# Deformable-convolution block: both horizontal weights of a sample applied on ScalarE, mixing one tap earlier, row combinations spread over the strip

## The chip, the cores and the metric

The kernel runs as one program on one core of a Trainium2 chip. A core has five engines that run on their own and meet only at semaphores: TensorE (PE, matmuls; PEld are its weight loads), VectorE (DVE), ScalarE (ACT), GpSimd (POOL) and SyncE (SP), which only issues transfers here. The metric is the device time of one execution in microseconds (us), lower is better.

## The reference, cut to what matters

```python
out_normal = _conv(x, w_normal)                      # x is (4, 128, 80, 80), all convolutions 3x3
offset = concatenate([_conv(x, w_offx), _conv(x, w_offy)], axis=1)
out_x = _deform_conv(x, offset, w_dx)
out_y = _deform_conv(x, offset, w_dy)
out = _conv(concatenate([out_normal, out_x, out_y], axis=1), w_fusion)
out = relu(_bn(out, ...bn1)); out = _bn(_conv(out, w_conv2), ...bn2)
return relu(out + x)

# _deform_conv, for each of 9 taps: a position per pixel, and the four cells around it
s = corner(y0i, x0i, (1 - ty) * (1 - tx)) + corner(y0i, x0i + 1, (1 - ty) * tx) \
  + corner(y0i + 1, x0i, ty * (1 - tx)) + corner(y0i + 1, x0i + 1, ty * tx)
return einsum('bckhw,ock->bohw', s, wr)              # zero outside the image
```

## The kernel before, in words

**Tiling.** The four images are cut into 40 strips of 8 rows (640 pixels, 5 tiles of 128). The 9 taps of all strips are numbered through: tap n = 9 * strip + k. A sample of a tap needs four cells; each tile of 128 pixels is fetched by one gather on POOL (L352, `cells`, 2 KB for each pixel, 45 gathers a strip, 1800 in all), into 15 slots that are used in turn. For the first image the gather reads `xpair` (upper and lower row of a cell pair); for images 2 to 4 it reads `slope_table`, which the kernel itself writes during the first image and which holds the upper row and the difference of lower and upper, so that one VectorE instruction does the vertical mix.

**A sample** is made so. First image: `upper` on ACT (L537, `mixed<-cells`, 5 instructions of 256 columns) times 1-ty, then the VectorE mix. All images: VectorE mixes vertically (L754, 5 instructions of 128x256, into `mixed`, two buffers), ACT multiplies the left half by 1-tx (L537, `samp<-mixed`, 5 of 128x128), VectorE adds the right half times tx (L760, 5 of 128x128). PE turns the five tiles (L433, into the one PSUM buffer `turned`), ACT takes the high part of the result (L536, `samp_hi`), VectorE the low part (L706, `samp_lo`), and PE multiplies the tap for both deformable convolutions (`deform_tap`, 36 matmuls into `acc`).

**The step.** `step(i)` is written once for each engine and runs 44 times (40 strips and 4 steps that empty the pipeline); it goes through the 9 taps. At tap n PE turns tap n+1, works off the slices of `SLICES[k]`, and then does `deform_tap` n. The slices are parts of the plain convolutions of other strips: O (offsets of strip i+1), F (fusion of strip i-2, in four quarters), N (normal convolution of strip i), C (second convolution of strip i-4). They share the two PSUM banks `work[0]` and `work[1]`, so a slice waits until ACT or VectorE has emptied its bank. At tap n VectorE makes sample n+2 (mix, then sum), then `samp_lo` n+1, then what the slices finished at this tap. ACT does the left products of n+2, `samp_hi` n+1, `upper` n+3, then its share of the finished slices. Each engine works its list off in the order written; nothing overtakes.

**Row combinations.** When the last quarter of F is done (tap 6), VectorE forms sums, differences and shifted differences of the rows of strip i-1 (L834, L835, L836, L840), the low part of `mid` (L919) and the low parts of the combinations (L706 twice), one after another, and ACT the high parts between them.

**What holds a gather.** Gather number q waits until the mix has freed its slot (at least q-14 mixes done) and until PE has marked progress (`pace`, 5 marks a tap; at least q-24 marks). The gathers of a strip also wait for its indices (`indices`, L723 to L740, 13 small VectorE instructions on the turned offsets), made at tap 3 of the strip before.

Of the kernel before, what the change touches and what calls it, by code (L numbers as in the profile page):

```python
# [15 lines left out]
TAPS = 9  # L16
EPS = 1e-5
ROWS = 8
# [44 lines left out]
STEPS = NS + 4  # L63


SLICES = [
# [41 lines left out]
class Flags:  # L108


    def __init__(self, i):
# [14 lines left out]
        self.turn = 2 if first else 3  # L126
# [19 lines left out]
def deform_block(nc, x, xflat, xpair, weights, bn, const, out):  # L146
    ctx = ExitStack()
    with ctx:
# [39 lines left out]
        resid = sb("resid", [128, 2, PIX])  # L188
# [3 lines left out]
        off_f = sb("off_f", [128, TILES, OFFC])  # L192
# [44 lines left out]
        sums_done, sums_hi, sums_lo = sem("sums_done"), sem("sums_hi"), sem("sums_lo")  # L237
        zs_done, zs_hi, zs_lo = sem("zs_done"), sem("zs_hi"), sem("zs_lo")
# [6 lines left out]
        resid_in = [sem("resid_in0"), sem("resid_in1")]  # L245
        out_ready = sem("out_ready")
        out_stored = [sem("out_stored0"), sem("out_stored1")]
# [15 lines left out]
        fuse_mid = resid[:, :, :].rearrange("p a n -> p (a n)")[:, 0:9 * C].rearrange("p (g k) -> p g k", g=3)  # L263
# [7 lines left out]
        def _(eng):  # L271
# [41 lines left out]
            def step(i, par, fl):  # L313
# [19 lines left out]
            for par in range(2):  # L333
                eng.wait_ge(out_stored[par], 16 * (NS // 2))
# [31 lines left out]
        def _(eng):  # L366
# [61 lines left out]
            def turn_samples(n, tp):  # L428

                at_least(eng, samp_done, TILES * n + TILES)  # L430
# [26 lines left out]
            def step(i, par, fl):  # L457
                early = i < FIRST_STEPS
                for k in range(TAPS):
# [9 lines left out]
                    for job, q, a, b in fl.slices[k]:  # L469
# [3 lines left out]
                        if a == 0 and job == "C":  # L473
# [4 lines left out]
                            if i - 1 < NS:  # L478
# [5 lines left out]
                        if a == 0 and job == "O":  # L484
                            if q == 0:
                                at_least(eng, x_lo_done, i + 2)
                            if not early:
                                at_least(eng, c_out, 2 * (i - 4) + q + 1)
                            elif i:
                                at_least(eng, n_out, 2 * (i - 1) + q + 1)  # L490
                            else:
                                at_least(eng, p_out, 1)
                        if a == 0 and job == "F":
                            if q == 0:
                                at_least(eng, w_lo_done, 1 + W_FUSE)
                                at_least(eng, sums_lo, i - 1)
                            if q == 2:
                                at_least(eng, zs_lo, i - 1)
# [4 lines left out]
                            if q < 2:  # L503
                                if not fl.nxt:
# [28 lines left out]
        def _(eng):  # L533
# [21 lines left out]
            def turned_evac(s):  # L555
                at_least(eng, p_done, s + 1)
                at_least(eng, idx_step, NIDX * (s - 1) + 2)
# [3 lines left out]
            def upper(n, c, k, par, tp):  # L561
                if c >= STRIPS:
                    return

                at_least(eng, samp_done, TILES * (n - 1))
                for j in range(TILES):
# [3 lines left out]
                         scale=wgt[:, par, 0, 0, j, k:k + 1]).then_inc(upper_done, 1)  # L570

            def left(n, k, par, tp):

                at_least(eng, samp_turned, n - 1)
# [25 lines left out]
            upper(0, 0, 0, 0, 0)  # L600
            left(0, 0, 0, 0)
            x_high(1, 1)
            upper(1, 0, 1, 0, 1)
            samples_high(0, 0)
            left(1, 1, 0, 1)
            upper(2, 0, 2, 0, 0)
# [5 lines left out]
            def rows_high(s):  # L612
# [382 lines left out]
```

## Time and profile before

| what | us |
|---|---|
| median of 3 runs (lowest, highest) | 2839.32 (2833.42, 2855.32) |
| the profiled execution | 2821.6 |
| its span, first to last instruction | 2819.8 |
| PE, PEld busy | 2410.5, 2374.3 |
| DVE busy | 2190.3 |
| POOL busy | 2160.5 |
| ACT busy | 1598.3 |

The profile is one execution; it took 0.6% less than the median of the runs. Busy is the time in which an engine has an instruction under way; an engine can be the bound with less than a full share if what it idles between two instructions is its own overhead. TensorE's granted clock was 0.933 of full speed in the mean.

### The profile page before, as it was taken

Reading aid. Unit: us, or ns where it says so; the run is one execution under the profiler, and the core shown is the slowest. Engines: PE = TensorE matmul, PEld = TensorE weight load, DVE = VectorE, ACT = ScalarE, POOL = GpSimd, SP = SyncE. Lnnn points to the kernel's source line nnn. Section 1 sums busy time; section 2 is a strip of 40 time slices with the busy share of each in tenths; the row PEclk is TensorE's granted clock in tenths of the full one; section 3 lists DMA queues with packets and bytes.
Section 4 is the critical chain, followed back from the end, with each engine's and each line's share of the span. In section 5 each row is a group of like instructions: output and inputs, shape, how many; then the busy total and the mean of one; then the engine's idle time right before and its main releaser. Section 6 shows DMA issues by size and latency. Waiting matters only on the chain.

```text
span 2819.8 us, 46173 instructions
## 1 busy us (share of the span) xinstructions
PE 2410.5 (85%) x15680; PEld 2374.3 (84%) x15680; DVE 2190.3 (78%) x5199; ACT 1598.3 (57%) x3577; POOL 2160.5 (77%) x1807
## 2 busy tenths in 40 slices
PE   3578889988988888888999888988999888888897
PEld 3577889888988888888998888988999888888897
DVE  5778778888877787777888877877878777778762
ACT  5777777877555555444555555555555555555541
POOL 7787777887777878888777788787777888777840
PEclk7789999999999999999999999999999999999999
DMA  7766777767766676666777766766666666666540
GB/s 228 210 209 209 218 223 214 218 208 217 215 219 215 198 232 205 202 201 199 221 229 221 224 198 211 230 184 192 197 199 194 180 184 184 191 198 206 175 135 20
DMA packets 179132, 564.84 MB, mean 200 GB/s; under 512 B 32720, under 2 KB 34128, under 8 KB 178768
## 3 DMA queue, kind: packets, MB, share of 16 engines
q0 software_dynamic: 144000, 471.97, 56.2%
q1 hardware_dynamic: 34896, 89.91, 9.1%
q8 instruction: 125, 2.05, 0.3%
q14 instruction: 111, 0.91, 0.1%
HBM read 527.41 MB, written 34.34 MB: 199 GB/s over the span
## 4 chain that ended last, share of the span: by engine, by line
PE 42%; DVE 24%; DMA 17%; issue 7%; ACT 5%; POOL 5%; ACTq 0%; POOLq 0%; DVEq 0%; SPq 0%
DMA cells<-slope_table,index 14%; PE work L390 9%; PE work L393 9%; PE work L396 9%; DVE mixed L754 5%; POOL cells L352 5%; PE turned L433 4%; DVE d_lo L706 4%; DVE samp L760 4%; PE acc L390 3%; PE acc L396 3%; PE acc L393 3%; DVE samp_lo L706 3%; DMA cells<-in_xpair,index 3%; DVE d_lo_f L836 2%
## 5 line engine op out<-in xcount | busy, mean ns | idle before, releaser
L352 POOL DMA_INDIRECT cells<-slope_table,index x1350 | 1627.7, 1206 | 411.3 <-issue 229.7
L537 ACT ACTIVATE samp<-mixed,wgt 128x128 f32<-128x128 f32 x1800 | 667.9, 401 | 784.7 <-DVE mixed L754 781.6
L754 DVE SCALAR_TENSOR_TENSOR mixed<-cells,wgt 128x256 f32<-128x256 f32 x1350 | 589.3, 479 | 324.8 <-DMA cells<-slope_table,index 322.2
L352 POOL DMA_INDIRECT cells<-in_xpair,index x450 | 523.1, 1162 | 144.9 <-issue 84.1
L433 PE MATMUL turned<-cst,samp 128*128 128x128 f32 x1800 | 283.9, 293 | 323.0 <-DVE samp_lo L706 302.1
L390 PE MATMUL work<-d_hi,w_hi 128*128 128x320 f32 x1440 | 475.5, 330 | 58.4 <-ACT off_s L536 52.2
L760 DVE SCALAR_TENSOR_TENSOR samp<-mixed,wgt,samp 128x128 f32<-128x128 f32 x1800 | 505.9, 344 | 21.6 <-ACT samp L537 21.2
L433 PEld LDWEIGHTS turned<-cst,samp 128*128 128x128 f32 x1800 | 229.3, 150 | 347.2 <-DVE samp L760 300.6
L393 PE MATMUL work<-d_lo,w_hi 128*128 128x320 f32 x1440 | 459.3, 319 | 0.0
L396 PE MATMUL work<-d_hi,w_lo 128*128 128x320 f32 x1440 | 458.8, 319 | 0.0
L390 PE MATMUL acc<-samp_hi,w_hi 128*128 128x320 f32 x1440 | 450.3, 313 | 1.0 <-DVE samp_lo L706 1.0
L393 PE MATMUL acc<-samp_lo,w_hi 128*128 128x320 f32 x1440 | 448.2, 311 | 0.0
L396 PE MATMUL acc<-samp_hi,w_lo 128*128 128x320 f32 x1440 | 448.0, 311 | 0.0
L706 DVE TENSOR_TENSOR samp_lo<-turned,samp_hi 128x640 fp32r<-128x640 f32 x360 | 294.1, 817 | 62.2 <-ACT samp_hi L536 61.3
L390 PEld LDWEIGHTS work<-d_hi,w_hi 128*128 128x128 f32 x1440 | 278.4, 193 | 68.2 <-ACT off_s L536 60.7
L536 ACT ACTIVATE samp_hi<-turned 128x640 fp32r<-128x640 f32 x360 | 249.2, 692 | 58.3 <-PE turned L433 56.2
L393 PEld LDWEIGHTS work<-d_lo,w_hi 128*128 128x128 f32 x1440 | 279.0, 194 | 0.0
L396 PEld LDWEIGHTS work<-d_hi,w_lo 128*128 128x128 f32 x1440 | 278.2, 193 | 0.0
L390 PEld LDWEIGHTS acc<-samp_hi,w_hi 128*128 128x128 f32 x1440 | 275.7, 191 | 1.2 <-DVE samp_lo L706 1.2
L393 PEld LDWEIGHTS acc<-samp_lo,w_hi 128*128 128x128 f32 x1440 | 274.4, 191 | 0.0
L396 PEld LDWEIGHTS acc<-samp_hi,w_lo 128*128 128x128 f32 x1440 | 273.4, 190 | 0.0
L390 PE MATMUL work<-x_hi,w_hi 128*128 128x320 f32 x720 | 259.7, 361 | 0.0
(89 smaller groups left out, 4166.8 us busy)
## 6 DMA issues: line engine op xcount, KB each, us to landing
cells<-slope_table,index POOLq DMA_INDIRECT x1350, 3.9
slope<-in_xpair SPq DMA_DIRECT2D x54, 384.0 KB, 5.6
slope_table<-slope SPq DMA_DIRECT2D x54, 384.0 KB
x_raw<-in_xflat SPq DMA_DIRECT2D x40, 410.0 KB, 4.3
resid<-in_x SPq DMA_DIRECT2D x40, 320.0 KB, 6.2
out<-resid SPq DMA_DIRECT2D x40, 320.0 KB, 4.0
cells<-in_xpair,index POOLq DMA_INDIRECT x450, 3.9
w_lo_f<-in_weights SPq DMA_DIRECT2D x4, 576.0 KB, 8.2
```

The source lines that it names most:

```text
L352: eng.indirect_dma_start(out=cells[:, g, :], out_offset=None, in_=cell_rows, in_offset=bass.IndirectOffsetOnAxis(ap=index[:, par, j, k:k + ...
L390: ins = eng.matmul(dst, w_hi[:, w], hi, start=start, stop=False, skip_group_check=True)
L393: ins = eng.matmul(dst, w_hi[:, w], lo, start=False, stop=False, skip_group_check=True)
L396: return eng.matmul(dst, w_lo[:, w], hi, start=False, stop=stop, skip_group_check=True)
L433: ins = eng.transpose(turned[:, j * 128:(j + 1) * 128], samp[:, tp, j, :], ident)
L536: return eng.activation(dst, src, ACT.Copy)
L537: return eng.activation(dst, src, ACT.Copy, scale=scale)
L706: return eng.tensor_tensor(dst, src, hi.bitcast(F32), ALU.subtract)
L754: eng.scalar_tensor_tensor(out=both, in0=corner[:, g, :, 1, :], scalar=wgt[:, par, 1, 0, j, k:k + 1], in1=base, op0=ALU.mult, op1=ALU.add, ...
L760: eng.scalar_tensor_tensor(out=samp[:, tp, j], in0=mixed[:, tp, j, C:2 * C], scalar=wgt[:, par, 1, 1, j, k:k + 1], in1=samp[:, tp, j], op0 ...
L836: eng.tensor_tensor(to[:, :, 1:Z_ROWS - 1, :], raw[:, :, 0:ROWS - 2, :], raw[:, :, 2:ROWS, :], ALU.subtract)\
```

## The change

- The descriptor scratch of the software-issued transfers (the gathers) goes from 4096 to 8192 bytes of each partition. To make room, `resid` has one buffer and not two, and the offset sum `off_f` is formed in place in `off_s`.
- For images 2 to 4 ACT makes both horizontal products, in place in `mixed` (10 instructions of 128x128 a tap, `across`), and VectorE adds the halves for all five tiles in one instruction of 128x640 (`blend`). The first image keeps the products and sums it had.
- At tap n VectorE does the sum of n+2, `samp_lo` n+1, and then the mix of n+3, one tap further ahead than before. ACT does `samp_hi` n+1 first, then the products of n+3 and `upper` n+4.
- The row combinations are spread: sums and differences at tap 4, their low part at tap 5, shifted differences at tap 6, their low part at tap 7. ACT's high parts move with them.
- From step 4 on the offsets O come first, whole, in tap 0; C follows in taps 0 to 2; F and N stand where they ended before. The offsets are turned at tap 1 (before 3). So C's first slice waits for the offsets' evacuation from the bank and not for N's.
- On SP the load of `resid` for a strip stands behind the store of the strip before and waits for it.

```diff
 SLICES = [
-    [("C", 0, 0, 9), ("C", 1, 0, 1)],
-    [("C", 1, 1, 9), ("O", 0, 0, 3)],
-    [("O", 1, 0, 3), ("F", 0, 0, 6)],
-    [("F", 0, 6, 9), ("F", 1, 0, 6)],
-    [("F", 1, 6, 9), ("F", 2, 0, 6)],
-    [("F", 2, 6, 9), ("F", 3, 0, 6)],
-    [("F", 3, 6, 9), ("N", 0, 0, 5)],
-    [("N", 0, 5, 9), ("N", 1, 0, 4)],
-    [("N", 1, 4, 9)],
+    [("O", 0, 0, 3), ("O", 1, 0, 3), ("C", 0, 0, 3)],
+    [("C", 0, 3, 9), ("C", 1, 0, 3)],
+    [("C", 1, 3, 9), ("F", 0, 0, 3)],
+    [("F", 0, 3, 9), ("F", 1, 0, 3)],
+    [("F", 1, 3, 9), ("F", 2, 0, 3)],
+    [("F", 2, 3, 9), ("F", 3, 0, 3)],
+    [("F", 3, 3, 9), ("N", 0, 0, 2)],
+    [("N", 0, 2, 9), ("N", 1, 0, 1)],
+    [("N", 1, 1, 9)],
 ]
...
-        self.turn = 2 if first else 3
+        self.turn = 2 if first else 1
...
-        resid = sb("resid", [128, 2, PIX])
+        resid = sb("resid", [128, PIX])
...
-                if fl.resid:
-                    s = i - 3
-                    slot = 1 - par
-                    at_least(eng, out_stored[slot], 16 * (s // 2))
-                    eng.dma_start(resid[:, slot], x[:, s * PIX:(s + 1) * PIX]).then_inc(resid_in[slot], 16)
                 if fl.second:
                     s = i - 4
                     at_least(eng, out_ready, 2 * s + 2)
-                    eng.dma_start(out[:, s * PIX:(s + 1) * PIX], resid[:, par]).then_inc(out_stored[par], 16)
+                    eng.dma_start(out[:, s * PIX:(s + 1) * PIX], resid[:]).then_inc(out_stored, 16)
+                if fl.resid:
+                    s = i - 3
+                    at_least(eng, out_stored, 16 * s)
+                    eng.dma_start(resid[:], x[:, s * PIX:(s + 1) * PIX]).then_inc(resid_in, 16)
...
-                            if i - 1 < NS:
+                            if fl.nxt and q == 0:
+                                at_least(eng, o_out, 2 * (i + 1) + 1)
+                            elif fl.nxt:
+                                at_least(eng, p_out, i + 2)
+                            elif i - 1 < NS:
                                 at_least(eng, n_out, 2 * (i - 1) + q + 1)
...
+            def across(n):
...
+                c, k, tp = n // TAPS, n % TAPS, n % 2
+                if n < PLAIN:
+                    at_least(eng, samp_turned, n - 1)
                 for j in range(TILES):
                     at_least(eng, mixed_done, TILES * n + j + 1)
-                    copy(samp[:, tp, j], mixed[:, tp, j, 0:C], scale=wgt[:, par, 0, 1, j, k:k + 1]).then_inc(left_done, 1)
+                    left, right = mixed[:, tp, j, 0:C], mixed[:, tp, j, C:2 * C]
+                    if n < PLAIN:
+                        copy(samp[:, tp, j], left, scale=wgt[:, c % 2, 0, 1, j, k:k + 1]).then_inc(left_done, 1)
+                    else:
+                        copy(left, left, scale=wgt[:, c % 2, 0, 1, j, k:k + 1]).then_inc(left_done, 1)
+                        copy(right, right, scale=wgt[:, c % 2, 1, 1, j, k:k + 1]).then_inc(left_done, 1)
...
-                    if fl.strip and k < TAPS - 2:
-                        left(n + 2, k + 2, par, tp)
...
                     if k == fl.turn and fl.nxt:
                         turned_evac(i + 1)
+                    across(n + 3)
+                    upper(n + 4)
...
+            def blend(n):
...
+                if n >= PLAIN:
+                    at_least(eng, samp_turned, n - 1)
+                    at_least(eng, left_done, left_count(n + 1))
+                    eng.tensor_tensor(samp[:, tp], mixed[:, tp, :, 0:C], mixed[:, tp, :, C:2 * C], ALU.add)\
+                        .then_inc(samp_done, 1)
+                    return
...
-                    if fl.strip and k < TAPS - 2:
-                        sample(n + 2, k + 2, par, tp)
...
+                    blend(n + 2)
                     if fl.strip and (k < TAPS - 1 or fl.nxt):
                         samples_low(n + 1, 1 - tp)
...
+                    mix(n + 3)
...
+                        if job == "F" and q == 1 and fl.rows:
+                            sums(i - 1)
...
+                        if job == "F" and q == 2 and fl.rows:
+                            sums_low(i - 1)
                         if job == "F" and q == T - 1:
...
                             if fl.rows:
-                                rows_combined(i - 1)
+                                zs(i - 1)
...
-                            if fl.rows:
-                                rows_low(i - 1)
+                        if job == "N" and q == 0 and fl.rows:
+                            zs_low(i - 1)
...
-    nc = bacc.Bacc("TRN2", target_bir_lowering=False, num_devices=1, dynamic_dma_scratch_size=4096)
+    nc = bacc.Bacc("TRN2", target_bir_lowering=False, num_devices=1, dynamic_dma_scratch_size=8192)
```

Two places of the order, in the middle of a strip of images 2 to 4. The first is VectorE's list from the last tap before the row combinations to the tap after them, before the change (L834 to L840 are the row combinations, L919 the low part of `mid`, L706 into `d_lo` the low parts, L870 a part of the slope table):

```order
L754 SCALAR_TENSOR_TENSOR mixed<-cells,wgt 128x256 x5
L760 SCALAR_TENSOR_TENSOR samp<-mixed,wgt,samp 128x128 x5
L706 TENSOR_TENSOR samp_lo<-turned,samp_hi 128x640
L870 TENSOR_TENSOR slope<-slope 128x3x128
L913 SCALAR_TENSOR_TENSOR mid_f<-work,minus,mid_f 128x4x80
L834 TENSOR_TENSOR d_lo_f<-raw 128x3x4x80
L835 TENSOR_TENSOR d_lo_f<-raw 128x3x4x80
L836 TENSOR_TENSOR d_lo_f<-raw 128x3x6x80
L840 TENSOR_TENSOR d_lo_f<-keep,raw 128x3x80
L919 SCALAR_TENSOR_TENSOR mid<-mid_f,mid 128x8x80
L706 TENSOR_TENSOR d_lo<-d_lo_f,d_hi 128x3x8x80
L706 TENSOR_TENSOR d_lo<-d_lo_f,d_hi 128x3x7x80
```

And the same list after it, from tap 4 to tap 6:

```order
L779 SCALAR_TENSOR_TENSOR mixed<-cells,wgt 128x256 x5
L948 SCALAR_TENSOR_TENSOR mid_f<-work,scale,mid_f 128x4x80
L950 SCALAR_TENSOR_TENSOR mid_f<-work,minus,mid_f 128x4x80
L875 TENSOR_TENSOR d_lo_f<-raw 128x3x4x80
L876 TENSOR_TENSOR d_lo_f<-raw 128x3x4x80
L792 TENSOR_TENSOR samp<-mixed 128x640
L728 TENSOR_TENSOR samp_lo<-turned,samp_hi 128x640
L779 SCALAR_TENSOR_TENSOR mixed<-cells,wgt 128x256 x5
L957 SCALAR_TENSOR_TENSOR mid_f<-work,scale,mid_f 128x4x80
L728 TENSOR_TENSOR d_lo<-d_lo_f,d_hi 128x3x8x80
L792 TENSOR_TENSOR samp<-mixed 128x640
L728 TENSOR_TENSOR samp_lo<-turned,samp_hi 128x640
```

The seven instructions that stood in one piece are now in four places, and between the mix and the next `samp_lo` there is one sum and not five. The second place is ACT's list from the end of a strip to tap 2 of the next, after the change:

```order
L549 ACTIVATE raw<-acc 128x320 x4
L549 ACTIVATE samp_hi<-turned 128x640
L550 ACTIVATE mixed<-mixed,wgt 128x128 x10
L549 ACTIVATE off_c<-work 32x320 x6
L549 ACTIVATE samp_hi<-turned 128x640
L549 ACTIVATE off_s<-work 128x270
L550 ACTIVATE mixed<-mixed,wgt 128x128 x10
L549 ACTIVATE d_hi<-d_lo_f 128x3x80
L710 ACTIVATE resid<-resid,scale 128x320
```

The evacuation of the offsets (`off_c`) stands behind the ten products of tap 0, in one piece, and every run of products stands behind the `samp_hi` of its own tap.

## Rows read from the trace of the kernel before

**Rows 1.** Page, costliest groups: busy, mean ns of one, idle before, its releasers.
```profile
L352 POOL DMA_INDIRECT cells<-slope_table,index x1350 | 1627.7, 1206 | 411.3 <-issue 229.7
L352 POOL DMA_INDIRECT cells<-in_xpair,index x450 | 523.1, 1162 | 144.9 <-issue 84.1
```

**Rows 2.** Windows, all engines: first image (late part), images 2 to 4.
```profile
381.60:678.50 296.90, 265.99 (x1747) 262.45 (x1747) 241.06 (x586) 232.52 (x550) 234.02 (x204) 0.95 0.72 223
678.50:2655.80 1977.30, 1746.57 (x11453) 1723.49 (x11452) 1580.31 (x3771) 1036.74 (x2280) 1578.46 (x1310) 0.95 0.67 204
```

**Rows 3.** Timeline of POOL: start, length, engine, line, operation, idle before and releaser.
```profile
886.45 8.75 POOL L352 DMA_INDIRECT cells<-slope_table,index  x1 [0.30 <-issue]
1642.00 8.75 POOL L352 DMA_INDIRECT cells<-slope_table,index  x1 [0.30 <-issue]
1651.06 2.99 POOL L352 DMA_INDIRECT cells<-slope_table,index  x1 [0.30 <-DVE mixed L754]
2655.78 9.53 POOL L352 DMA_INDIRECT cells<-slope_table,index  x1 [0.30 <-PE work L390]
```

**Rows 4.** Timeline of DVE at 1642: the row combinations and what follows.
```profile
1641.20 1.15 DVE L834 TENSOR_TENSOR d_lo_f<-raw 128x960 f32<-128x960 f32 x1
1649.85 2.06 DVE L754 SCALAR_TENSOR_TENSOR mixed<-cells,wgt 128x256 f32<-128x256 f32 x5
```

**Rows 5.** Timeline, POOL then DVE, at another strip's row combinations.
```profile
1030.81 2.32 POOL L352 DMA_INDIRECT cells<-slope_table,index  x1 [0.30 <-PE acc L390]
1033.43 2.81 POOL L352 DMA_INDIRECT cells<-slope_table,index  x1 [0.30 <-issue]
1036.55 1.52 POOL L352 DMA_INDIRECT cells<-slope_table,index  x1 [0.31 <-issue]
...
1032.23 0.40 DVE L840 TENSOR_TENSOR d_lo_f<-keep,raw 128x240 f32<-128x240 f32 x1
```

**Rows 6.** Timeline of POOL beside the mixes of other taps.
```profile
1523.97 3.26 POOL L352 DMA_INDIRECT cells<-slope_table,index  x1 [0.30 <-DVE mixed L754]
1615.29 0.95 POOL L352 DMA_INDIRECT cells<-slope_table,index  x1 [0.30 <-DVE mixed L754]
```

**Rows 7.** Timeline of DVE at those two places.
```profile
1523.03 2.06 DVE L754 SCALAR_TENSOR_TENSOR mixed<-cells,wgt 128x256 f32<-128x256 f32 x5
1526.32 0.82 DVE L706 TENSOR_TENSOR samp_lo<-turned,samp_hi 128x640 fp32r<-128x640 f32 x1
1615.41 0.48 DVE L754 SCALAR_TENSOR_TENSOR mixed<-cells,wgt 128x256 f32<-128x256 f32 x1 [0.18 <-DMA cells<-slope_table,index]
```

**Rows 8.** Timeline of ACT, then of DVE: a tap's chain, and a mix with its product.
```profile
1609.44 1.58 ACT L537 ACTIVATE samp<-mixed,wgt 128x128 f32<-128x128 f32 x5
1611.04 0.70 ACT L536 ACTIVATE samp_hi<-turned 128x640 fp32r<-128x640 f32 x1
1636.86 0.40 ACT L537 ACTIVATE samp<-mixed,wgt 128x128 f32<-128x128 f32 x1 [1.14 <-DVE mixed L754]
...
1611.78 0.82 DVE L706 TENSOR_TENSOR samp_lo<-turned,samp_hi 128x640 fp32r<-128x640 f32 x1 [0.19 <-ACT samp_hi L536]
1636.34 0.48 DVE L754 SCALAR_TENSOR_TENSOR mixed<-cells,wgt 128x256 f32<-128x256 f32 x1 [1.05 <-DMA cells<-slope_table,index]
```

**Rows 9.** Timeline of DVE: first and last of the 13 index instructions.
```profile
1620.06 0.24 DVE L723 TENSOR_TENSOR off_f<-off_s 128x90 f32<-128x90 f32 x1
1623.03 0.25 DVE L740 TENSOR_SCALAR index<-above,cst 128x45 int32<-128x45 f32 x1
```

**Rows 10.** Lines by form: busy, mean ns, idle before; left products and offsets.
```profile
L537 ACT ACTIVATE samp<-mixed,wgt 128x128 f32<-128x128 f32 x1800 | 667.9, 401 | 784.7 <-DVE mixed L754 781.6
L536 ACT ACTIVATE off_c<-work 32x320 f32<-32x320 f32 x240 | 101.9, 425 | 9.3 <-PE work L375 7.0
```

**Rows 11.** DMA issues of the page: KB each, median us to landing.
```profile
resid<-in_x SPq DMA_DIRECT2D x40, 320.0 KB, 6.2
out<-resid SPq DMA_DIRECT2D x40, 320.0 KB, 4.0
```

More of the change, by code:

```diff
@@ L332, in _ @@
             run_steps(eng, step)
-            for par in range(2):
-                eng.wait_ge(out_stored[par], 16 * (NS // 2))
+            eng.wait_ge(out_stored, 16 * NS)
             eng.wait_ge(slope_stored, 16 * SLOPES)
@@ L486, in step @@
                                 at_least(eng, x_lo_done, i + 2)
[L487 to L489 removed]
+                            if i:
                                 at_least(eng, n_out, 2 * (i - 1) + q + 1)
@@ L503, in step @@
                             if q < 2:
-                                if not fl.nxt:
+                                if fl.second:
                                     at_least(eng, c_out, 2 * (i - 4) + q + 1)
@@ L599, in _ @@
             weights_high(W_DEF)
-            upper(0, 0, 0, 0, 0)
-            left(0, 0, 0, 0)
+            upper(0)
+            across(0)
             x_high(1, 1)
-            upper(1, 0, 1, 0, 1)
+            upper(1)
+            across(1)
+            upper(2)
             samples_high(0, 0)
-            left(1, 1, 0, 1)
-            upper(2, 0, 2, 0, 0)
+            across(2)
+            upper(3)
             eng.wait_ge(bn_step, 1)
@@ L625, in step @@
                     tp = (par + k) % 2
-                    if fl.strip and k < TAPS - 2:
-                        left(n + 2, k + 2, par, tp)
-                    elif fl.strip and fl.nxt:
-                        left(n + 2, k + 2 - TAPS, 1 - par, tp)
                     if fl.strip and (k < TAPS - 1 or fl.nxt):
@@ L633, in step @@
                         weights_high(fl.weights[k])
-                    if fl.strip and k < TAPS - 3:
-                        upper(n + 3, i, k + 3, par, 1 - tp)
-                    elif fl.strip and fl.nxt:
-                        upper(n + 3, i + 1, k + 3 - TAPS, 1 - par, 1 - tp)
                     if k == fl.turn and fl.nxt:
                         turned_evac(i + 1)
+                    across(n + 3)
+                    upper(n + 4)
                     if k == 1 and fl.last_row:
@@ L686, in step @@
                             at_least(eng, c_out, 2 * s + q + 1)
-                            part = resid[:, par, q * HALF:(q + 1) * HALF]
+                            part = resid[:, q * HALF:(q + 1) * HALF]
                             eng.activation(part, part, ACT.Relu, bias=scale1[:, 3:4]).then_inc(out_ready, 1)
@@ L741, in indices, with mix @@
                 eng.wait_ge(idx_ready, s + 1)
-            def sample(n, k, par, tp):
+            def mix(n):
+                if n >= TOTAL:
+                    return
+                c, k, tp = n // TAPS, n % TAPS, n % 2
                 for j in range(TILES):
@@ L799, in _ @@
             weights_low(W_DEF)
-            sample(0, 0, 0, 0)
+            mix(0)
+            blend(0)
             x_low(1, 1)
-            sample(1, 1, 0, 1)
+            mix(1)
+            blend(1)
             samples_low(0, 0)
+            mix(2)
             eng.wait_ge(bn_in, 16)
@@ L877, in step @@
                         last_row(i - 2)
-                    if fl.strip and k < TAPS - 2:
-                        sample(n + 2, k + 2, par, tp)
-                    elif fl.strip and fl.nxt:
-                        sample(n + 2, k + 2 - TAPS, 1 - par, tp)
+                    blend(n + 2)
                     if fl.strip and (k < TAPS - 1 or fl.nxt):
@@ L904, in step @@
                                                      op0=ALU.mult, op1=ALU.add).then_inc(f_two, 1)
+                        if job == "F" and q == 1 and fl.rows:
+                            sums(i - 1)
                         if job == "F" and q == 2 and fl.fuse:
@@ L930, in step @@
                             if q == 0:
-                                at_least(eng, resid_in[par], 16 * (s // 2) + 16)
-                            part = resid[:, par, q * HALF:(q + 1) * HALF]
+                                at_least(eng, resid_in, 16 * s + 16)
+                            part = resid[:, q * HALF:(q + 1) * HALF]
                             eng.scalar_tensor_tensor(out=part, in0=work[q][:, 0:HALF], scalar=scale1[:, 2:3],
```

92 lines of the change are left out of this document (53 added, 39 removed).

## The prediction

> **What bounds the kernel now.** I read the busy shares first and they name nobody: TensorE is busiest, and four engines are within a fifth of each other. So I went to the idle time before the costliest groups. POOL's gathers idle 411.3 + 144.9 = 556.2 us over 1800 instructions, 0.31 us before each [rows 1], and the timeline shows the same 0.30 before a quick gather and before one that follows a stall [rows 3, 6]: up to its last gather POOL never waits for a free slot or for TensorE's pace. It is the bound. A strip of images 2 to 4 takes 45 * 1977.3 / 1310 = **67.9 us**, one of the late first image 45 * 296.9 / 204 = **65.5 us** [rows 2].
>
> An undisturbed gather is 0.95 long [rows 6], so 45 of them with their gaps are 45 * 1.25 = 56.3 us. The mean gather of images 2 to 4 is 1.206 long [rows 1]: 45 * (1.206 - 0.95) = 11.5 us a strip are stalls inside gathers. They come from VectorE. The gather of 1642.00 lasts 8.75 and ends 0.90 after the first mix behind the row combinations starts [rows 3, 4]; elsewhere 2.32 ends 0.90 after L840 starts [rows 5], and 3.26 ends 0.91 after `samp_lo` starts, behind an unbroken run of five mixes and five sums [rows 6, 7]. A gather that meets a mix standing alone, since VectorE itself waits for cells, is not delayed [rows 6, 7]. A gather thus waits while VectorE works without a gap on operands in SBUF, sometimes over several instructions. Gathers over 8 us stand in 15 of the 30 strips of images 2 to 4, and in none before (the first and the last of them in [rows 3]). Such a strip loses 7.8 + 2.0 = 9.8 at its row combinations [rows 3], one like [rows 5] 1.4 + 1.9 + 0.6 = 3.8. In the mean that is 6.8; the other 4.7 us a strip, 0.52 a tap, fall on the mixes and sums.
>
> **The change, part by part: POOL.** The row combinations keep their instructions, but in pieces of at most about 4 us. I price them as the strip of [rows 5], 3.8, where the lock was let go between instructions; bounds 2.8 (a quarter less, since each piece also begins with POOL free) and 6.8 (as now). At a tap five sums, 1.2 us (1525.09 to 1526.32, [rows 7]), become one of about 0.82 (a two-input instruction of 640 columns takes that, [rows 7]), and the run of mixes then ends in a gap, as VectorE waits for ACT's products. Bounds for a tap are 0.3 and 0.52; I take 0.43, nearer the old value because a single long instruction can't be interrupted: 3.9 a strip. POOL's own time becomes 56.3 + 3.8 + 3.9 = **64.0 us** (bounds 61.8 and 67.8), 3.9 less than now.
>
> The Trainium skill, page "SBUF — State Buffer", section "Who interferes with whom", says that a VectorE instruction with two SBUF inputs contends with a GpSimd instruction that reads SBUF and that the one which comes first has the shared ports for the whole instruction. By that rule alone a gather waits for one instruction at most, and cutting a run in pieces buys nothing. The 8.75 us over seven instructions [rows 3, 4] says that a gather can also miss the boundaries. What the rule would make of the time is the second rival below.
>
> **A new chain between ACT and VectorE.** Before, ACT's list had slack: its products waited 781.6 us for mixes [rows 10]. Now a tap's `samp_hi` n+1, VectorE's `samp_lo` n+1, its first mix of n+3 and ACT's ten products of n+3 follow one another, and ACT can do nothing in between. `samp_lo` starts 0.74 after `samp_hi`, lasts 0.82, and a product starts 0.52 after its mix [rows 8]; less the 0.70 of `samp_hi`, ACT stands 1.38 us a tap. For images 2 to 4, a strip on ACT:
> - busy now: 67.9 * 1036.7 / 1977.3 = 35.6 [rows 2], less 45 left products of 0.371 (667.9 / 1800, [rows 10]) = 18.9
> - 90 products: five take 1.58, so one starts every 0.295 and ten take 3.06 [rows 8]: 27.5 a strip
> - 9 * 1.38 = 12.4
> - at tap 1 the index chain, 1620.06 to 1623.28 [rows 9], now lies before the mix: 3.2, less 0.4 of evacuation that runs beside `samp_lo`: 2.8
> - at tap 4 ACT's high part waits for the sums behind five mixes and two evacuations: about 1.5
> - at tap 0 TensorE waits for `off_c` before C, then has 9 matmuls of C, 12 of the deformable tap and 5 transposes until ACT's next `samp_hi`: 26 * 0.1525 (1746.57 / 11453, [rows 2]) = 4.0, beside which ACT has three of its six `off_c` of 0.425 [rows 10]: 2.7 of waiting
>
> The sum is **65.8 us**. Its terms that rest on rows alone are firm; the three waits could be 2 less if VectorE and TensorE run ahead, or 2 more if cells come late: 63.8 to 67.8.
>
> TensorE, 60.0 busy a strip [rows 2], gets a wait at tap 0: the four `acc` copies (priced as `off_c`, the same 320 columns), `samp_hi`, 1.38, the products and three `off_c` are 1.7 + 0.7 + 1.4 + 3.1 + 1.3 = 8.2 us, it has 23 instructions (3.5) beside them, so 4.7, in all 64.7. VectorE, 1580.3 / 1977.3 * 67.9 = 54.3 busy, loses 9 * (1.23 - 0.82) = 3.7 and binds nowhere.
>
> Three chains stand at 64.0, 65.8 and 64.7, coupled more tightly than before: gathers may still run only 24 ahead of TensorE's marks, but the mix now takes them one tap earlier, so about five gathers of lead are left where there were ten. I give them 0.2 above the longest: **66.0 us** a strip, 1.9 less than now, 30 * 1.9 = 57 us.
>
> **First image.** The work is unchanged there, the order is not. ACT is busy 65.5 * 232.5 / 296.9 = 51.3 a strip [rows 2]; with 12.4, 2.8, 2.7 and about 0.5 at tap 4 its chain is 69.7, above the 65.5 at which POOL ran. That holds for the six strips with the new slices: +25 us. The first four strips lack C and most of F, and stay POOL's: 0.
>
> **Small parts.** One `resid` buffer: in the middle of the kernel the store and the load, 4.0 + 6.2 us to landing [rows 11], have over 50 us until the next use. At the very end the load of the last strip follows the store before it, about 10 us against a step of about 10 in which it was hidden: +5, between 0 and 10. The larger scratch: every stall of a gather ends at a VectorE boundary, so I see none that is a full ring: 0, and below nothing only if the 0.30 or 0.95 themselves hold such a wait. In-place offset sum: 0, the same 13 instructions. With the stalls gone, ACT's products are late next.
>
> **Sum.** 2821.6 - 57 + 25 + 5 = 2795 us against the profiled execution. The median of the runs is 0.6% above it, so **2812 us** in runs, 1.0% below 2839.3. About 1% is what a measurement of this kernel can tell from no change, so the forecast sits on that line.
>
> **The rivals.**
> - *Forecast, 0.45:* 65.3 to 66.7 us a strip, 2790 to 2835.
> - *The lock costs as much in pieces, 0.22.* The rule quoted above, as a mechanism here: each piece of 1 to 2 us stops the gather that meets it, and the sum of 0.82 holds each tap's. POOL stays at 67.9, the first image and the end cost their 30: 2821.6 + 30, times 1.006, is 2869, 1% slower. For it: in [rows 5] single instructions took 1.4 and 1.9. Against: the 8.75 of [rows 3].
> - *ACT's chain binds, slower, 0.13.* Place: the ten products behind each `samp_hi`. It decides from 68 us a strip, that is if products start every 0.33 instead of 0.295 or VectorE's late jobs push `samp_lo`. At 69.5 in images 2 to 4 and 72 in the first: 48 + 39 + 5 = 92, so 2930.
> - *Stalls nearly vanish, 0.18.* Gathers at 62 and the three waits on ACT at their lower end, 64: 30 * 3.9 = 117 less, plus 25: 2730 * 1.006, about 2745. For it: mixes with gaps delay no gather [rows 6, 7].
> - *The scratch does something, 0.02:* if the 0.30 or the 0.95 fell, ACT's chain would hold the time at about the former case.
>
> **How the numbers follow.** Faster by over 1% is below 2811: the case of vanishing stalls, 0.18, the scratch, 0.02, and nearly half of the forecast's, 0.22: 0.42. Slower by over 1% is above 2868: ACT's chain, 0.13, and a good half of the lock's, 0.13: 0.26. Within 1%: 0.32. The range leaves out the slow chain's upper part and the fastest tail: 2745 to 2895.
>
> **What the profile after would show.** The idle before gathers should rise above 0.30, with TensorE or the mix as releaser, since POOL no longer binds alone; no gather over 8 us; mean gather about 1.12 us in images 2 to 4. ACT's largest idle should be before the products, near 1.3 us each time, and TensorE should stand about 4 us at tap 0 behind `off_c`. Wrong would be: gathers still back to back at a mean near 1.2 (the lock is not cheaper), or ACT's products starting at another distance than 0.295.

## The result and the profile after

The changed kernel takes **2908.4 us** in the median (2901.6 to 2915.1, 4 runs), the kernel before beside it 2836.4 (2809.1 to 2855.3, 4 runs): a ratio of 1.029 with a 95% interval of 1.021 to 1.037. It is slower by 3%, where 2812 was forecast, and above the range of 2745 to 2895. The profiled executions have spans of 2912.5 and 2819.8. One of the four executions of experiment 4 below took 4876.4 us at a granted clock of 0.523 and stays out of that experiment's ratio.

First the costliest groups of the page after, which answer to [rows 1] and [rows 10] (busy, mean ns of one, idle before them and its releaser):

```profile
L364 POOL DMA_INDIRECT cells<-slope_table,index x1350 | 1572.2, 1165 | 493.5 <-issue 196.6
L550 ACT ACTIVATE mixed<-mixed,wgt 128x128 f32<-128x128 f32 x2700 | 826.3, 389 | 524.8 <-DVE mixed L779 524.2
L364 POOL DMA_INDIRECT cells<-in_xpair,index x450 | 507.3, 1127 | 226.6 <-issue 78.7
L387 PE MATMUL work<-x_hi,w_off 128*128 128x328 f32 x480 | 175.2, 464 | 183.3 <-DVE x_lo L728 183.3
```

The gathers themselves are shorter, as the change meant them to be, but POOL now idles 720.1 us around them and not 556.2: it is no longer the bound. The offsets' matmuls (O) idle 183.3 us for `x_lo`, once a strip. The windows say where the time is (the last three columns are granted clock, DMA share, GB/s; the gathers are the last count in brackets):

```profile
18.00:298.00 280.00, 171.47 (x983) 164.22 (x983) 196.67 (x478) 193.65 (x444) 202.05 (x180) 0.79 0.66 197
381.60:678.50 296.90, 246.94 (x1554) 240.74 (x1553) 214.01 (x516) 211.31 (x490) 202.87 (x180) 0.91 0.64 195
760.00:2600.00 1840.00, 1608.79 (x10405) 1585.39 (x10404) 1300.55 (x2486) 1206.03 (x3274) 1395.86 (x1196) 0.93 0.66 202
```

The first of these windows in the kernel before, which [rows 2] don't have:

```profile
18.00:298.00 280.00, 181.64 (x1097) 175.19 (x1097) 213.67 (x509) 201.50 (x472) 221.78 (x192) 0.84 0.69 209
```

A strip takes 45 * 280 / 180 = 70.0 us in the first four (45 * 280 / 192 = 65.6 before), 74.2 in the late first image (65.5 before, [rows 2]) and 45 * 1840 / 1196 = 69.2 in images 2 to 4 (67.9 before; 66.0 forecast). By POOL's timelines the first gather of strip 10 starts at 744 and not 678, +66, and the last of all at 2808.2 and not 2716.3. So images 2 to 4 take 26 us more (57 less was forecast), the first image 66 more (25), and the end about 1 more (5).

Within a strip, one tap holds most of the error. From one `samp_hi` to the next, images 2 to 4 take 9.1 us at tap 1, 5.4 at taps 2 and 3, 8.3 to 8.5 at tap 4, 4.9 at tap 5, about what the terms of the prediction make; tap 6 takes 9.6. **Tap 0 takes 13.0 in the mean** (5.9 before), where these terms give 0.7 + 1.4 + 3.1 + 2.6 + 2.7 = 10.5. In the mean over strips 10 to 38 the products start 2.0 behind `samp_hi`, as forecast, but take 4.35 and not 3.1 from first to last; the first three `off_c` take 1.3; and from the start of C to the next `samp_hi` it is 5.3 and not 26 * 0.1525 = 4.0. Here is one such tap on ACT (start, length, line, operation, idle before it and releaser):

```profile
1342.51 0.87 ACT L549 ACTIVATE x_hi<-x_raw 128x820 fp32r<-128x820 f32 x1
1343.28 1.41 ACT L549 ACTIVATE raw<-acc 128x320 f32<-128x320 f32 x4
1344.55 0.73 ACT L549 ACTIVATE samp_hi<-turned 128x640 fp32r<-128x640 f32 x1
1346.57 2.44 ACT L550 ACTIVATE mixed<-mixed,wgt 128x128 f32<-128x128 f32 x8 [1.28 <-DVE mixed L779]
1350.68 0.69 ACT L550 ACTIVATE mixed<-mixed,wgt 128x128 f32<-128x128 f32 x2 [1.67 <-DVE mixed L779]
1351.28 2.62 ACT L549 ACTIVATE off_c<-work 32x320 f32<-32x320 f32 x6
1358.08 0.71 ACT L549 ACTIVATE samp_hi<-turned 128x640 fp32r<-128x640 f32 x1 [4.18 <-PE turned L445]
```

The same stretch on PE and, below it, the mix that made ACT wait at 1350, on DVE:

```profile
1344.48 0.92 PE L387 MATMUL work<-x_hi,w_off 128*128 128x328 f32 x2 [4.24 <-DVE x_lo L728]
...
1352.71 0.61 PE L402 MATMUL work<-mid,w_hi 128*128 128x320 f32 x1 [3.18 <-ACT off_c L549]
```

```profile
1350.16 0.48 DVE L779 SCALAR_TENSOR_TENSOR mixed<-cells,wgt 128x256 f32<-128x256 f32 x1 [2.44 <-DMA cells<-slope_table,index]
```

POOL beside it:

```profile
1354.07 0.94 POOL L364 DMA_INDIRECT cells<-slope_table,index  x1 [1.71 <-PE work L402]
1356.47 0.94 POOL L364 DMA_INDIRECT cells<-slope_table,index  x1 [1.46 <-PE acc L402]
```

And PE's granted clock in four pieces of it (length, PE busy, clock, DMA share, GB/s):

```profile
1339.60:1344.40 4.80, 0.65 (x6) 0.78 0.66 192
1344.48:1349.50 5.02, 5.02 (x18) 0.54 0.91 313
1352.71:1355.70 2.99, 2.99 (x11) 0.50 0.41 126
1356.01:1358.00 1.99, 1.99 (x17) 1.00 0.24 95
```

O waits 4.24 us for `x_lo`, then C waits 3.18 for `off_c`. After the first wait O's 18 matmuls run at about 1.2 GHz and take 5.0 us; after the second C starts at 1.2 GHz too and is at 2.4 only from 1356 on. `off_c` begins 6.7 us after `samp_hi`, behind the ten products, and the last two of these are late because the mix has no cells: POOL's gathers just before stand 0.30 apart, so it has no lead left. While C waits, PE marks no progress, and POOL stands for 1.71 and 1.46.

### The profile page after: what moved, and what is told of

It reads as the page before. It is cut to its first block, busy times and chain, and to the rows that moved or that the text cites. A ratio compares the mean times of both kernels' runs of the same rounds, so it can differ in the third digit from the quotient of the medians.

```text
span 2912.5 us, 46443 instructions
## 1 busy us (share of the span) xinstructions
PE 2454.1 (84%) x15680; PEld 2409.5 (83%) x15680; DVE 2025.4 (70%) x4119; ACT 1903.5 (65%) x4927; POOL 2089.1 (72%) x1807
## 4 chain that ended last, share of the span: by engine, by line
DVE 35%; ACT 30%; PE 11%; issue 11%; DMA 9%; POOL 3%; ACTq 0%; DVEq 0%; SPq 0%; POOLq 0%
ACT mixed L550 15%; DVE mixed L779 12%; DMA cells<-slope_table,index 8%; DVE samp_lo L728 7%; ACT samp_hi L549 5%; POOL cells L364 3%; ACT samp L550 3%; PE work L402 3%; DVE d_lo L728 2%; PE work L408 2%; PE work L405 2%; ACT off_c L549 2%; DVE d_lo_f L876 1%; DVE samp L792 1%; PE acc L402 1%
## 5 line engine op out<-in xcount | busy, mean ns | idle before, releaser
L364 POOL DMA_INDIRECT cells<-slope_table,index x1350 | 1572.2, 1165 | 493.5 <-issue 196.6
L550 ACT ACTIVATE mixed<-mixed,wgt 128x128 f32<-128x128 f32 x2700 | 826.3, 389 | 524.8 <-DVE mixed L779 524.2
L364 POOL DMA_INDIRECT cells<-in_xpair,index x450 | 507.3, 1127 | 226.6 <-issue 78.7
L779 DVE SCALAR_TENSOR_TENSOR mixed<-cells,wgt 128x256 f32<-128x256 f32 x1350 | 562.3, 477 | 89.1 <-DMA cells<-slope_table,index 87.9
L402 PE MATMUL work<-d_hi,w_hi 128*128 128x320 f32 x1440 | 466.0, 324 | 10.5 <-ACT mid_f L672 6.1
L445 PE MATMUL turned<-cst,samp 128*128 128x128 f32 x1800 | 263.9, 278 | 147.0 <-DVE samp_lo L728 129.2
L445 PEld LDWEIGHTS turned<-cst,samp 128*128 128x128 f32 x1800 | 217.2, 143 | 167.4 <-issue 157.2
L402 PE MATMUL work<-mid,w_hi 128*128 128x320 f32 x720 | 248.1, 345 | 110.1 <-ACT off_c L549 100.2
L387 PE MATMUL work<-x_hi,w_off 128*128 128x328 f32 x480 | 175.2, 464 | 183.3 <-DVE x_lo L728 183.3
L792 DVE TENSOR_TENSOR samp<-mixed 128x640 f32<-128x640 f32 x270 | 221.7, 821 | 119.5 <-ACT mixed L550 95.5
L387 PEld LDWEIGHTS work<-x_hi,w_off 128*128 128x128 f32 x480 | 132.7, 309 | 192.3 <-DVE x_lo L728 185.3
```

Of the source, the lines that this page charges most:

```text
L364: eng.indirect_dma_start(out=cells[:, g, :], out_offset=None, in_=cell_rows, in_offset=bass.IndirectOffsetOnAxis(ap=index[:, par, j, k:k + ...
L387: ins = eng.matmul(work[half][:, 0:HR * PITCH], w_off[:, ky, w].rearrange("p g n -> p (g n)"), part[:, par, rows, :], start=(n == 0), stop ...
L402: ins = eng.matmul(dst, w_hi[:, w], hi, start=start, stop=False, skip_group_check=True)
L445: ins = eng.transpose(turned[:, j * 128:(j + 1) * 128], samp[:, tp, j, :], ident)
L550: return eng.activation(dst, src, ACT.Copy, scale=scale)
L779: eng.scalar_tensor_tensor(out=both, in0=corner[:, g, :, 1, :], scalar=wgt[:, c % 2, 1, 0, j, k:k + 1], in1=base, op0=ALU.mult, op1=ALU.ad ...
```

## The experiments

The experiments ran in three groups of four, each group on one chip beside the kernel before, whose median there was 2827, 2826 and 2827 us (experiments 1 to 4, 5 to 8, 9 to 12). Ratios are to the kernel before on the same chip, with 95% intervals. Times of different groups come from different chips, and a difference of 10 us between two of them is not told apart from none.

**1. Offsets back at taps 1 and 2.** The change with the old table of slices and its waits.

```diff
-    [("O", 0, 0, 3), ("O", 1, 0, 3), ("C", 0, 0, 3)],
-    [("C", 0, 3, 9), ("C", 1, 0, 3)],
...
+    [("C", 0, 0, 9), ("C", 1, 0, 1)],
+    [("C", 1, 1, 9), ("O", 0, 0, 3)],
...
-        self.turn = 2 if first else 1
+        self.turn = 2 if first else 3
```

> The change with the offsets of the next strip back at taps 1 and 2 (turned at tap 3), all else as changed. Theory (the loss sits at tap 0: x_lo, then O, then off_c, then C, each waiting for the one before): tap 0, from one samp_hi to the next, falls from about 14 us to about 7.5, taps 1 to 3 together grow by about 3; a strip of images 2 to 4 falls from 69.3 to about 66, one of the first image from 74 to about 68, and the time to about 2780 us (2750 to 2820). Rival (the ten products behind each samp_hi, or the gathers, hold the strip wherever O stands): tap 0 falls but the other taps grow by as much, 2880 to 2910.

Measured: **2796.2 us**, 0.990 (0.982 to 0.998). Tap 0 falls to 6.1 us, taps 1 to 3 together grow by 3.7. Its windows:

```profile
18.00:298.00 280.00, 170.08 (x983) 162.98 (x983) 196.60 (x477) 193.48 (x444) 200.92 (x180) 0.80 0.65 197
381.60:678.50 296.90, 254.60 (x1645) 246.43 (x1644) 227.94 (x548) 222.34 (x516) 214.01 (x190) 0.96 0.66 204
760.00:2600.00 1840.00, 1641.33 (x10975) 1591.40 (x10975) 1375.71 (x2610) 1270.02 (x3444) 1456.36 (x1260) 0.99 0.69 211
```

That is 65.7 us a strip in images 2 to 4, close to the 66.0 forecast, but 70.0 and 70.3 in the first image. The offsets' place, with the slices moved along with it, costs 112 us; the first image has another loss. In images 2 to 4 POOL is back to back again (413.3 us idle over 1350 gathers, 0.306 each), and VectorE waits 98.2 us for its cells, 3.3 a strip:

```profile
L364 POOL DMA_INDIRECT cells<-slope_table,index x1350 | 1560.2, 1156 | 413.3 <-issue 245.3
L778 DVE SCALAR_TENSOR_TENSOR mixed<-cells,wgt 128x256 f32<-128x256 f32 x1350 | 567.4, 478 | 100.7 <-DMA cells<-slope_table,index 98.2
```

**2. Offsets first alone,** in the kernel before (the slices, their waits and `turn` as in the change, nothing else).

> The kernel before with nothing but the new order of TensorE's work (offsets of the next strip at tap 0, turned at tap 1, C after them, the jobs spread more evenly). Theory (tap 0): TensorE stands about 4 us before O in every strip and again before C, and the strip becomes 1 to 3 us longer: about 2900 us (2865 to 2950). Rival (the order alone costs nothing, ACT's products do): 2836 within 15.

Measured: 2869.0 us, 1.013 (1.005 to 1.021), 42 us and not 112. PE's waits are there, but behind `samp_hi` ACT has only `upper` or nothing before `off_c`. Tap 0 is 11.6 long in the late first image, where five `upper` copies stand there (5.7 before), and 7.1 in images 2 to 4, where nothing does (5.9 before). So the new place is dear where a run of copies or products stands between `samp_hi` and `off_c`.

**3. The small parts alone,** in the kernel before (scratch of 8192 bytes, one `resid`, offset sum in place).

> The kernel before with the three small parts alone: a scratch of 8192 bytes, one resid buffer, the sum of the offsets in place. Both theories: 2836 plus 0 to 10 us, the gathers as before (1.19 mean, 0.30 between). If it is over 2860, the small parts carry a part of the 72 us, which neither theory has.

Measured: 2795.2 us, 0.987 (0.979 to 0.995). A gain that neither theory had; see 8 and 12.

**4. Left product alone on ACT,** all else as changed: `across` makes five products in every image, `blend` five sums.

> The change with only the left product on ACT and five sums of two operands a tap on VectorE, as before the change; the mixing stays a tap ahead, the row combinations spread and the offsets first. Theory (tap 0): tap 0 stays at 12 us or more although ACT has 45 products fewer a strip; the time falls little, to about 2880 (2850 to 2900). Rival (ACT's ten products hold the strip): the strip falls by 3 us or more, 2830 or less.

Measured: 2861.2 us, 1.011 (1.001 to 1.021): 47 us less than the change, not the 78 of the rival. Tap 0 is 11.9 in images 2 to 4, not 13.0. Fewer products shorten the way to `off_c`, which already spoke for ACT's list.

**5. First image in the old order,** on top of 1.

```diff
+                    if n + 2 < PLAIN:
+                        across(n + 2)
                     if fl.strip and (k < TAPS - 1 or fl.nxt):
                         samples_high(n + 1, 1 - tp)
...
-                    across(n + 3)
-                    upper(n + 4)
+                    if n + 3 >= PLAIN:
+                        across(n + 3)
+                    upper(n + 3)
```

VectorE's `mix` moves in the same way.

> The kernel with the offsets back at taps 1 and 2, and in the first image also the old order of the products (mixing in the tap itself, not a tap ahead; the later images mix a tap ahead). Theory (mixing a tap ahead takes five gathers of lead, and in the first image ACT's wide copies of a later tap stand in front of everything else): the first image's strips fall from 70 to 75 us to about 66.5, the later ones stay at 64.8 to 67.1; about 2755 us (2740 to 2775). Rival (the first image is slow through the spread row combinations or the one resid buffer): about 2796, no change.

Measured: **2737.4 us**, 0.971 (0.965 to 0.977), more than expected. POOL's waits between 82 and 298 us, in the change and then here (total, times, longest):

```profile
POOL cells L364 <- PE acc L405: 19.6, 5, 7.1
POOL cells L364 <- DVE mixed L779: 10.0, 26, 1.2
```

```profile
POOL cells L364 <- issue: 29.0, 95, 0.3
POOL cells L364 <- DVE mixed L779: 9.5, 31, 0.3
```

With mixing ahead in the first image POOL waits up to 7.1 us for PE's marks; in the old order no wait is over the usual 0.3.

**6. Offsets from the strip at hand.** As changed, but O reads a strip whose `x_lo` is long ready; the offsets are the neighbour strip's.

```diff
-                                at_least(eng, x_lo_done, i + 2)
+                                at_least(eng, x_lo_done, i + 1)
...
-                            offsets(1 - par, q)
+                            offsets(par, q)
```

> The changed kernel with the offsets first, but computed from the strip at hand, which lies ready, instead of the next one (the offsets of a strip are those of its neighbour; as many instructions of the same sizes). It takes away only TensorE's wait for x_lo at tap 0. Theory (x_lo, O, off_c and C in a row make tap 0 long): TensorE doesn't stand before O, tap 0 falls from 13.6 to 14.2 us to about 10.4, its length by ACT's own list; 3.5 us a strip less, about 2800 us (2780 to 2830). Rival (the wait for off_c before C is the whole loss, and ACT's products set its time): tap 0 stays over 12.5, the time over 2860.

Measured: 2926.5 us, 1.039 (1.033 to 1.045). **My theory fell here**, the rival was right: tap 0 is 13.6 in images 2 to 4. PE's timeline at the same strip:

```profile
1342.85 0.56 PE L387 MATMUL work<-x_hi,w_off 128*128 128x328 f32 x2 [1.26 <-ACT raw L549]
1352.58 0.60 PE L402 MATMUL work<-mid,w_hi 128*128 128x320 f32 x1 [8.12 <-ACT off_c L549]
```

O is done before `samp_hi` of 1344.75, and C still starts where it did, 1352.58: it waits 8.12 us for `off_c`, which ACT begins at 1351.14, behind its products. The wait for `x_lo` was hidden behind the later one; it was not the cause.

**7. Row combinations spread alone,** in the kernel before: `sums` behind the second quarter of F, their low part behind the third, `zs` behind the last, its low part behind N's first half.

> The kernel before with the row combinations spread over three taps, nothing else. Theory (a gather gets between the pieces, as the prediction priced it: stalls fall from 11.7 to about 8.7 us a strip, no gather over 8 us, and POOL's gathers set the strip): 65 us a strip, about 2750 us (2730 to 2790). Rival (the pieces cost the gathers as much, or TensorE, ACT and VectorE hold the strip at the same length): 2815 to 2850.

Measured: **2749.9 us**, 0.978 (0.971 to 0.985). POOL's longest gather behind strip 9 is 3.52 us (before 9.5); POOL first, then DVE beside it:

```profile
1608.03 3.52 POOL L352 DMA_INDIRECT cells<-slope_table,index  x1 [0.31 <-PE acc L390]
1611.86 1.67 POOL L352 DMA_INDIRECT cells<-slope_table,index  x1 [0.30 <-DVE mixed L759]
```

```profile
1608.03 1.65 DVE L845 TENSOR_TENSOR d_lo_f<-raw 128x1440 f32<-128x1440 f32 x1
1609.60 0.40 DVE L849 TENSOR_TENSOR d_lo_f<-keep,raw 128x240 f32<-128x240 f32 x1
1609.91 0.82 DVE L937 SCALAR_TENSOR_TENSOR mid<-mid_f,mid 128x640 fp32r<-128x640 f32 x1
1610.65 2.06 DVE L759 SCALAR_TENSOR_TENSOR mixed<-cells,wgt 128x256 f32<-128x256 f32 x5
```

The gather ends 0.90 after the first mix starts, over three instructions: the piece as a whole holds it, as the whole block did in [rows 3, 4], and shorter pieces hold it for less.

**8. One `resid` and the sum in place, scratch at 4096.**

> The kernel before with one resid buffer and the sum of the offsets in place, the scratch at 4096 bytes as before. It tells what the three small parts together (1.3% faster than before) owe to the scratch. If the scratch did it, this runs as before, 2825 to 2840. If the scratch does nothing, it runs like the three together, about 2795; if that gain was an accident of where gathers meet VectorE's runs, anywhere from 2795 to 2835 with the same mean of an undisturbed gather (0.948) and the same 0.305 between gathers.

Measured: 2785.3 us (10 runs), 0.990 (0.986 to 0.994), as 3. The scratch does nothing that can be measured.

**9. Half of `off_c` ahead of the products,** all else as changed.

```diff
+                    if k == 0 and i >= FIRST_STEPS and fl.nxt:
+                        off_evac(i + 1, 0)
                     across(n + 3)
                     upper(n + 4)
...
-                        if job == "O" and fl.nxt:
+                        if job == "O" and fl.nxt and (q or i < FIRST_STEPS):
```

> The changed kernel, offsets first, but ACT copies the first half of off_c at tap 0 ahead of its ten products instead of behind them. Theory, after the run with x ready (TensorE's wait moved from O to C, since off_c stands on ACT behind acc, x_hi, samp_hi and the ten products): C starts when O ends, about 4.5 us after samp_hi instead of 6.3 to 9, tap 0 falls from 13.6 to 14.2 us to about 10.5; about 2800 us (2780 to 2840). Rival (x_lo and a slow O come first, ACT then waits for O with its products behind it): no gain, 2880 or more.

Measured: **2797.6 us**, 0.992 (0.989 to 0.994), the time of experiment 1 with the offsets still first. ACT at the same strip:

```profile
1288.68 0.73 ACT L549 ACTIVATE samp_hi<-turned 128x640 fp32r<-128x640 f32 x1
1291.48 1.30 ACT L549 ACTIVATE off_c<-work 32x320 f32<-32x320 f32 x3 [2.07 <-PE work L387]
1292.81 3.06 ACT L550 ACTIVATE mixed<-mixed,wgt 128x128 f32<-128x128 f32 x10
1295.89 1.31 ACT L549 ACTIVATE off_c<-work 32x320 f32<-32x320 f32 x3
1298.06 0.70 ACT L549 ACTIVATE samp_hi<-turned 128x640 fp32r<-128x640 f32 x1 [0.86 <-PE turned L445]
```

ACT even stands 2.07 us for O, which has waited 5.86 for `x_lo` and starts its matmuls 0.27 apart, and the tap is 9.4 long all the same. With PE's wait before C gone the cells are no longer late either: the ten products take 3.1 in the mean and not 4.35, and POOL's idle before a gather is back at 0.306.

**10. Spread and small parts,** in the kernel before: no second product, no mixing ahead, offsets at taps 1 and 2.

> The kernel before with the row combinations spread and the three small parts; both products, one sum, mixing ahead and offsets first are left out. If the two gains add up (2750 for the one, 1.0 to 1.3% for the other): about 2720 us (2705 to 2735), and the products on ACT have brought nothing, since the best so far with them has 2737. If not: 2740 to 2760, and the products bring a little.

Measured: 2730.6 us, 0.968 (0.965 to 0.972), within the range given for gains that add up.

**11. Experiment 5 with five products and five sums a tap.**

> The best version so far (offsets at taps 1 and 2, old order in the first image, 2737 us) with the left product alone on ACT and five sums of two operands a tap on VectorE; mixing a tap ahead stays in the later images. Theory of the prediction (one sum of 0.82 stalls the gathers 0.1 us a tap less than five of 1.2): 0.8 us a strip more, about 2760 us (2750 to 2780). Rival (ACT's ten products lengthen the chain from samp_hi to the next by more than the shorter sum gains): 2735 or less.

Measured: **2727.6 us**, 0.967 (0.964 to 0.971), the fastest here, 10 us below experiment 5, which ran on another chip. POOL is back to back in both, and its gathers are no longer here than in 5. First experiment 11, then 5:

```profile
L364 POOL DMA_INDIRECT cells<-slope_table,index x1350 | 1542.6, 1143 | 411.3 <-issue 208.4 <-DVE mixed L774 136.2 <-PE acc L402 36.0
```

```profile
L364 POOL DMA_INDIRECT cells<-slope_table,index x1350 | 1553.7, 1151 | 411.5 <-issue 259.4 <-DVE mixed L779 108.5 <-PE acc L402 22.9
```

The mean gather is 8 ns shorter, 11 us over 1350 gathers. So what difference there is lies in the gathers, and the rival's reason, a longer chain on ACT, is not shown: POOL waits for nothing in either.

**12. The offset sum in place alone.**

> The kernel before with only the sum of the offsets in place (ACT's copy of the turned offsets then waits for one more of VectorE's steps). If the gain of the small parts comes from the one resid buffer, this runs as before, 2815 to 2840; if it comes from here, about 2790.

Measured: 2823.1 us (10 runs), 0.997 (0.994 to 1.001), no change. So what is left for the 1% of 3 and 8 is the one `resid` buffer, whose load now stands behind the store; it was not run alone.

**The whole way,** each step from one kernel to the next: before 2827; spread, -77 (7), or -63 by its ratio of 0.978; small parts, -19 (10); mixing ahead in images 2 to 4, -3, no difference (11); both products on ACT and one sum, +10, no more than two chips may differ by (5); mixing ahead in the first image, +59 (1); offsets first, +112 (the change).

## Why the prediction was wrong

**POOL is the bound before, through stalls in its gathers.** Right. Spreading the row combinations alone gives 2.2%, and with POOL back to back in images 2 to 4 (experiments 1, 5, 7, 9, 10, 11) the time follows its mean gather: 45 * (1.151 + 0.305) = 65.5 us a strip in experiment 5, where the windows give 65.4. No gather over 8 us is left, and the products start at 0.3 us, as said. The rival that the lock costs the same in pieces fell with experiment 7. The Trainium skill, page "SBUF — State Buffer", section "Who interferes with whom", gives the ports to the earlier instruction for the whole of that one instruction. The gather of 3.52 us stands over three VectorE instructions, so here the trace does not agree.

**Stalls of 7.7 us a strip after the change.** Too low: the mean gather of 1.165 makes 45 * (1.165 - 0.95) = 9.7. The term of the taps was mis-sized: I took 0.1 us a tap off for one sum of 0.82 in place of five of 1.2, but the gathers are 1.151 long with the one sum and 1.143 with the five. That accounts for about 1 of the 2.0 us; where the rest lies, in the pieces or in the mixes, was not separated. The second product on ACT bought nothing.

**ACT's chain, 65.8 us.** Its regular part came as summed: 1.28 + 0.74 around ten products in 3.04, the index chain at tap 1, the sums at tap 4. Missed was tap 6, 9.6 long: the low part of the sums stands before `samp_lo`, and ACT waits 2.3 for the mix and not 1.28, about 1.1 a strip. The 65.7 a strip with the offsets moved back doesn't confirm the sum. There POOL is back to back, 45 * (1.156 + 0.306) = 65.8, and VectorE waits 3.3 us a strip for cells, so ACT's chain would have let the strip be shorter. That the two numbers agree is luck.

**Tap 0: "2.7 of waiting" on ACT, 4.7 on TensorE, and 0.2 for the thinner lead.** This is the step that failed. The path was right: C needs `off_c`, `off_c` stands behind the products, these need cells, and the next `samp_hi` needs C and the deformable tap. This ring makes the 10.5. Two of its terms were too small. I priced the 26 matmuls from C on at 0.1525 each, which is a mean at a clock of 0.95 ([rows 2]), though they come right behind a wait; the first eleven start 0.27 apart, and the stretch takes 5.3 and not 4.0. And I priced the thinner lead of gathers at 0.2 for the whole strip; at tap 0 alone late cells make the products 1.25 longer. Together the ring takes 13.0 instead of 10.5, 2.5 of the 3.2 us by which a strip of images 2 to 4 is too long, and 13.6 in the late first image. The two overruns hang together: experiment 9 cuts the ring at `off_c`, the cells come in time again, and 110 us come back; experiment 6 cuts it at `x_lo` and gets nothing. That PE would stand at tap 0 behind `off_c` was forecast, and it did, for 3.2 us here. The 4.2 before O were not forecast, and by experiment 6 they cost nothing.

**First image: 0 for four strips, 69.7 for the rest.** The second step that failed, for 41 us of the error. The early strips were left at POOL's 65.6 and take 70.0. Mixing ahead is the cause: without it they are back at 65.6 (experiment 5, 192 gathers in 280 us). `samp_hi`, 1.3 us of waiting, five left products and five wide `upper` copies make a regular tap of 6.2 there, 4.2 before and in experiment 5. ACT's chain by the prediction's own terms would not have said so: 65.6 * 201.5 / 280 = 47.2 busy, with 12.4, 2.8 and 0.5, is 62.9. What these terms lack is POOL's standing of 5.1 to 7.1 us for PE's marks, once a strip. How the loss divides between ACT's list and POOL's shorter lead is open, since experiment 5 takes away both. The late strips are at 70.3 without the offsets' move, so 69.7 was a fair sum, and tap 0 adds 4 more.

**Small parts, +5.** The wrong sign: one `resid` buffer gains about 1%. Scratch 0 and sum in place 0 were right. What the buffer changes is not settled: an undisturbed gather is as long as before and the gap the same 0.30, only fewer long stalls show (in experiment 8, 5 gathers over 8 us and not 15, mean 1.160 instead of 1.206).

**The rival that came true** is the slower one, "ACT's chain binds", given 0.13, with 69.5 and 72 us a strip against 69.2 and 74.2. Its price of 92 us against the 93 measured is luck: it put 48 on images 2 to 4 and 39 on the first, where 26 and 66 were measured. Of the two mechanisms named for it, the products kept their distance of 0.295; `samp_lo` was late at tap 6, for about 1.1 us a strip. Most of the loss is at tap 0, behind the products.

## What to carry to other kernels

Where two engines hand work to each other within one tap, write the ring of hand-overs in order, and don't price its parts by means over the whole kernel: the matmuls behind a wait go at the low clock, and what needs gathers with no lead left is late. When a job is moved ahead, its evacuation has to move ahead with it; here three copies of 0.43 us before ten products instead of behind them were worth 110 us. And try the parts of a bundle alone: of this one, spreading the row combinations gave 2.2%, and the offsets' place and mixing ahead in the first image took back nearly twice what it and the small parts had given.

## What the runs showed that was not expected

- A wait removed from the front of a ring (4.24 us before O) reappears at the next place (8.12 before C, against 3.18), and the time doesn't fall.
- A TensorE wait can cost twice: after 4.2 and 3.2 us of standing, the matmuls that follow start 0.27 us apart instead of 0.15, at a granted clock of 0.54 and 0.50.
- In experiments 1, 5 and 9 POOL is the bound again in images 2 to 4, though ACT's ten products stand in the chain. Of the whole change only the ring at tap 0 took that bound away there.
- One buffer in place of two, with its load behind the store instead of before it, seems to make the kernel 1.0% faster (0.986 to 0.994, with the offset sum in place, which alone shows no change), and no reason for it was found.
